# Softmax and window sums of the second half shared between VectorE and GpSimd in a gated spectral convolution kernel

## The chip, the cores and the metric

One core of a Trainium2 chip. The metric is the device time of one execution in microseconds. The engines are TensorE (PE in the rows; PEld is its weight load), VectorE (DVE), ScalarE (ACT), GpSimd (POOL) and SyncE (SP). Each works through its own list of instructions in order; semaphores tie them together.

## The reference

```python
# x: 32 images, 128 channels, 16 x 16
x = x + kan_gate(gn(x))              # gate per image and channel from the mean over pixels
z = gn(x)                            # group norm again
r = conv1x1(relu(conv1x1(relu(conv1x1(z, rw_fc1)), rw_conv)), rw_fc2)
routeing = softmax(r.mean((2, 3)).reshape(B, NF=4, MED=256), axis=1)
s = conv3x3(relu(conv3x3(z, sp_fc1)), sp_fc2)
spatial_routeing = softmax(s.mean((2, 3)).reshape(B, 4, 256), axis=1)
xp = star_scale * relu(z @ w_pw1.T) ** 2 + star_bias
xf = rfft2(xp)
weight         = einsum('bfc,hwf->bhwc', routeing, complex_weights)
spatial_weight = einsum('bfc,hwf->bhwc', spatial_routeing, spatial_weights)
out = xp * spatial_weight + irfft2(xf * weight)
x = x + out @ w_pw2.T
```

The mean over pixels of the second 3x3 convolution is linear, so it needs no convolution: for each of nine taps it needs the sum of the hidden image over the window that the tap sees. That window leaves out an edge row, an edge column or both.

## The kernel before, in words

The 32 images are two halves of 16. A prologue computes group statistics and the gate. Then the branches run over groups of four images (it = 0 to 7): `taps` (L1285) on TensorE are the 3x3 convolution and the first 1x1, ScalarE rectifies them (`conv_hidden`, `route_hidden`, `second_hidden`) and leaves sums over pixels. After a half, its routing is computed:

- `edges` on VectorE (L973 to L975): sums over edge rows and columns, and the corners, of the hidden images.
- `windows` and `window_corners` on VectorE (L987 to L990, L1001): 8 and 4 subtractions of 128 x 8 elements that make the sums of the nine windows.
- `image_sums` (for the second half on ScalarE, L652): copies them, scaled, into the layout that the matmuls read, once for each of two rows of images (g = 0, 1).
- `logits(half)` on TensorE: 32 matmuls of tap pairs (L1350), the last tap (L1354) on partitions 64 to 127, and the route branch (L1357, in the second half L1362) on partitions 0 to 63. ScalarE copies the result out (`logits_copy`), TensorE turns it (`turn_logits`, L1187), VectorE adds the bias (L1046).
- softmax over the four filters: the maximum (L1054), its subtraction, the exponential (ScalarE, L642), the sum (L1064), its reciprocal (L1065), the scaling, and the split of the shares into three bf16 parts (`own_part`, `left_of`).

Then the image loop: one round for each image, `round_of(i)` on each engine. A round of TensorE is, in order, `waves_onto(i)` (L1408), `compose(i-1)` (L1471), `waves_of(i+1)` (L1397), `prime` (L1416), `mix(i+2)` (L1429, L1432), in odd rounds `turn_route` (L1449), `expand(i+3)` (L1384), `reduce(i)` (L1460). VectorE: `products(i)` (L1123, L1124), `even_sum(i+2)` (L1092), `finish(i-2)` (L1128), `terms(i+1)` (L1112 to L1114), `spatial(i+2)` (L1099). ScalarE: `folded_copy(i-1)` (L708, L710), `slot_mix`, in odd rounds `route_copy`, `rectified`, `y_copy(i)`, `square`. GpSimd: `fold(i)` (L457, L458), `unfold(i-2)` (L464, L465), `odd_sum(i+2)` (L451). Rounds 0 to 13 are unrolled and rounds 14 to 29 are in a hardware loop.

The rounds of the first half start while the second half's routing is still to be made. Its steps stand in the unrolled rounds, after the round's own work, at places written by hand: a table `extras` on VectorE and ScalarE, `if` lines on GpSimd and TensorE. Those places set the order, since each engine keeps to it. What waits on them: `products` waits for `waves_onto`; `waves_onto(i)` waits for `terms(i)` and both halves of `fold(i)`; `spatial(i)` waits for `fold(i-1)`; `turn_route(2)`, in round 1, writes bank 7 and so waits for `folded_copy(0)`, which reads it.

In the second half `logits(1)` writes the convolution part to columns 0 to 255 of bank 6 and the route part to columns 256 to 511 of the same bank. The two run on different partitions of the array's rows, so one waits for the other:

```python
if half:
    last.then_inc(conv_logits, 1)
    pe.wait_ge(conv_logits, 1)
    for f in range(NF):
        last = mm(bank[6][NB * f:NB * f + NB, MED:2 * MED], r2_p[:, :], rwf_t[:, f, :], start=True, stop=True)
```

## Time and profile before

| | us |
|---|---|
| median of 3 runs | 253.31 |
| the 3 runs | 251.72 to 256.84 |
| the profiled execution | 252.96 |
| its span, first to last instruction | 251.2 |
| TensorE busy | 230.0 (92%) |
| VectorE busy | 203.2 (81%) |
| ScalarE busy | 147.4 (59%) |
| GpSimd busy | 125.3 (50%) |

The times of the rows count from the start of the span. The profiled execution took 252.96 us as a whole, its span 251.2, so 1.76 us lie around the span. An engine's busy share is a mean over stages with different limits: the branches up to about 92 us, the unrolled rounds to about 172, the loop after them.

### The profile page before, as it was taken

What the parts mean: (1) busy time and instruction counts of PE and PEld (TensorE: products, weight loads), DVE (VectorE), ACT (ScalarE), POOL (GpSimd) and SP (SyncE); (2) the same over time, 40 slices, a digit from 0 to 9 for tenths busy, and PEclk for the clock granted to TensorE, in tenths of its full rate; (3) what the DMA queues carried; (4) which work ended last, traced back from release to release, by engine and by line L of the source; (5) the groups of instructions that cost most, each with busy time, mean ns of one, the idle gap of its engine ahead of it and who ended that gap; (6) DMA issues with size and microseconds to landing.
All of it is one profiled execution on the core that took longest, in us unless ns stands there. A gap on an engine that the chain in (4) does not pass through costs nothing.

```text
span 251.2 us, 6925 instructions
## 1 busy us (share of the span) xinstructions
PE 230.0 (92%) x2257; PEld 180.9 (72%) x2257; DVE 203.2 (81%) x534; ACT 147.4 (59%) x359; POOL 125.3 (50%) x213
## 2 busy tenths in 40 slices
PE   0597889999999999959999989999999999999994
PEld 0597755555444545848788888998989898989983
DVE  3988999982967824886499899899898989989873
ACT  2034386845974866646365756766666675756641
POOL 1532360220000011635467677988686868778771
PEclk9999999999999999979999999999999999999999
DMA  7999500000000000000000010100101010101011
GB/s 214 361 301 274 237 3 3 1 1 3 3 3 0 3 0 1 4 1 22 14 29 23 21 44 22 44 23 30 37 21 42 21 42 21 42 21 42 23 42 63
DMA packets 9483, 13.19 MB, mean 52 GB/s; under 512 B 732, under 2 KB 8924, under 8 KB 9332
## 3 DMA queue, kind: packets, MB, share of 16 engines
q1 hardware_dynamic: 9428, 12.80, 16.1%
q8 instruction: 14, 0.23, 0.4%
q10 hardware_dynamic: 32, 0.08, 0.3%
q14 instruction: 9, 0.07, 0.1%
HBM read 8.69 MB, written 4.19 MB: 51 GB/s over the span
## 4 chain that ended last, share of the span: by engine, by line
PE 71%; DVE 14%; issue 5%; DMA 3%; POOL 3%; ACT 3%; SPq 1%; DVEq 0%; ACTq 0%; POOLq 0%
PE bank L1285 19%; PE bank L1408 10%; PE bank L1460 10%; PE bank L1397 9%; PE bank L1384 7%; PE bank L1471 4%; DMA x_all<-in_x 3%; PE bank L1416 2%; PE bank L1217 1%; PE bank L1350 1%; PE bank L1300 1%; PE bank L1449 1%; DVE x_all L1128 1%; DVE stats L814 1%; PE bank L1429 1%
## 5 line engine op out<-in xcount | busy, mean ns | idle before, releaser
L451 POOL TENSOR_TENSOR eo<-xp 128x256 f32<-128x256 f32 x32 | 23.7, 739 | 70.0 <-ACT xp L682 70.0
L1285 PE MATMUL bank<-z_all,split_h 128*64 128x480 f16 (+2 forms) x320 | 37.5, 374 | 1.0 <-ACT z_all L573 1.0
L1408 PE MATMUL bank<-later_sb,qt_eo 128*128 128x128 f32 x256 | 35.1, 279 | 1.9 <-DVE bank L1113 1.4
L1460 PE MATMUL bank<-later_sb,prod 128*128 128x128 f32 x256 | 34.8, 280 | 0.4 <-DVE prod L1124 0.4
L1397 PE MATMUL bank<-later_sb,eo 128*128 128x128 f32 x256 | 33.9, 276 | 0.0
L1408 PEld LDWEIGHTS bank<-later_sb,qt_eo 128*128 128x128 f32 x256 | 31.3, 192 | 3.6 <-DVE bank L1113 2.0
L1460 PEld LDWEIGHTS bank<-later_sb,prod 128*128 128x128 f32 x256 | 31.8, 196 | 1.4 <-DVE prod L1124 0.6
L689 ACT ACTIVATE w_slot<-bank 128x512 f32<-128x512 f32 x32 | 19.1, 597 | 22.5 <-PE bank L1432 22.5
L1397 PEld LDWEIGHTS bank<-later_sb,eo 128*128 128x128 f32 x256 | 31.1, 192 | 0.4 <-issue 0.4
L457 POOL TENSOR_TENSOR qt_eo<-qt 128x256 f32<-128x256 f32 x32 | 28.5, 890 | 3.3 <-PE bank L1408 2.6
L1285 PEld LDWEIGHTS bank<-z_all,split_h 128*64 128x64 f16 x320 | 17.3, 110 | 16.1 <-issue 3.1
L458 POOL TENSOR_TENSOR qt_eo<-qt 128x256 f32<-128x256 f32 x32 | 28.6, 894 | 0.0
L1128 DVE SCALAR_TENSOR_TENSOR x_all<-x_all,coef,waves 128x256 f32 (+1 forms) x31 | 27.7, 893 | 1.0 <-POOL waves L465 1.0
L1099 DVE SCALAR_TENSOR_TENSOR qt<-xp,shift,bank 128x512 f32<-128x512 f32 x32 | 23.5, 733 | 5.0 <-PE bank L1429 3.6
L675 ACT ACTIVATE relu_v<-bank,relu_scale 128x512 f32<-128x512 f32 x32 | 22.0, 688 | 4.5 <-PE bank L1384 3.7
L1123 DVE TENSOR_TENSOR prod<-bank,t_im 128x256 f32<-128x256 f32 x32 | 13.5, 422 | 13.6 <-PE bank L1408 13.4
L1217 PE MATMUL bank<-early_sb 128*128 128x128 f32 x102 | 15.5, 311 | 9.2 <-DMA x_all<-in_x 9.2
L1384 PE MATMUL bank<-split_h,z_all 128*128 128x256 f16 x128 | 23.4, 279 | 0.0
L1112 DVE TENSOR_TENSOR bank<-bank,w_slot 128x504 f32<-128x504 f32 x32 | 21.7, 679 | 1.0 <-PE bank L1416 0.9
L708 ACT ACTIVATE folded<-bank,coef 128x128 f32<-128x128 f32 x31 | 11.4, 366 | 18.0 <-PE bank L1471 17.7
L1092 DVE SCALAR_TENSOR_TENSOR eo<-xp,shift 128x256 f32<-128x256 f32 x32 | 19.1, 598 | 3.3 <-ACT xp L682 3.3
L1114 DVE TENSOR_TENSOR t_im<-bank,w_slot 128x504 f32<-128x504 f32 x32 | 21.3, 667 | 0.0
(188 smaller groups left out, 470.1 us busy)
## 6 DMA issues: line engine op xcount, KB each, us to landing
x_all<-in_x SPq DMA_DIRECT2D x8, 512.0 KB, 9.0
out<-x_all SPq DMA_DIRECT2D x32, 128.0 KB, 1.7
sp_t<-in_branch_s SPq DMA_DIRECT2D x1, 2560.0 KB, 15.9
later_sb<-in_later SPq DMA_DIRECT2D x1, 918.5 KB, 9.1
sym_all<-in_sym SPq DMA_DIRECT2D x1, 292.5 KB
early_sb<-in_early SPq DMA_DIRECT2D x1, 278.0 KB, 3.8
rwf_t<-in_branch_r SPq DMA_DIRECT2D x1, 256.0 KB, 13.6
kan_sb<-in_kan ACTq DMA_DIRECT2D x1, 80.8 KB, 3.5
```

The lines of the kernel that those rows point to most:

```text
L451: pool.tensor_tensor(eo[p][:, 1, :], xp[p][:, 0, :], xp[p][:, 1, :], ALU.subtract).then_inc(odd_ready, 1)
L457: pool.tensor_tensor(qt_eo[:, 0, :], qt[:, 0, :], qt[:, 1, :], ALU.add).then_inc(q_folded, 1)
L458: pool.tensor_tensor(qt_eo[:, 1, :], qt[:, 0, :], qt[:, 1, :], ALU.subtract).then_inc(q_folded, 1)
L675: act.activation(relu_v[:, :], bank[0], ACT.Relu, scale=relu_scale[:, 0:1]).then_inc(relu_ready, 1)
L1099: dve.scalar_tensor_tensor(out=qt[:, :, :], in0=xp[p], scalar=shift[:, 0:1], in1=mixed_pixel, op0=ALU.add, op1=ALU.mult).then_inc(qt_ready, 1)
L1112: tt(total[:, :, :, 2:P], spec[:, :, :, 2:P], w[:, :, 0, 2:P].unsqueeze(2).broadcast_to(wide_shape), ALU.mult).then_inc(re_ready, 1)
L1128: dve.scalar_tensor_tensor(out=one(x_all, i), in0=one(x_all, i), scalar=one(coef[:, 0, :].unsqueeze(2), i), in1=waves[:, :, :].rearrange(" ...
L1285: last = mm(dst[:, :, rows_out, cols_out], w[:, t, :], pixels(z_all[:, b:b + 2, part, :])[:, :, rows_in, cols_in], start=(n == 0 and t in ...
L1384: last = mm(bank[0][:, t * MED:(t + 1) * MED], z[:, part, cols], w, start=(n == 0), stop=(n == 2))
L1397: last = mm(spec[:, m, :, 64 * odd:64 * odd + 64], eo[p][:, odd, m * P:(m + 1) * P], forward[:, odd, :, :], start=True, stop=True)
L1408: last = mm(total[:, m, :, 64 * odd:64 * odd + 64], qt_eo[:, odd, m * P:(m + 1) * P], forward[:, odd, :, :], start=False, stop=(odd == 1 a ...
L1460: last = mm(bank[1][:, odd * C:(odd + 1) * C], prod[:, m, odd].rearrange("p a s -> p (a s)"), pw2_t[:, m, :], start=(m == 0), stop=(m == 1))
```

## The change

For the second half alone:

- VectorE's `edges(7, 8)` moves from the end of round 0 to just ahead of `spatial(1)`, which precedes round 0. The 8 subtractions of `windows` and the 4 of the corners go from VectorE to GpSimd: 8 between `odd_sum(1)` and `odd_sum(2)`, 4 between `fold(1)` and `odd_sum(3)`. `fold(0)` now stands ahead of `odd_sum(1)`.
- ScalarE copies both rows of images (`image_sums(0)`, `image_sums(1)`) at the end of round 0. The second stood at the end of round 1.
- `logits(1)` writes the route part to bank 7, each of its matmuls beside one of the last tap's, which stays in bank 6. The wait between them is gone. New are waits for `folded_copy(1)` and the third route copy ahead of `logits(1)`, and one for both logits copies ahead of `compose(2)` in round 3.
- The maximum is found at the end of round 4 and no longer of round 3. GpSimd takes it off in one operation, and no longer two. The exponential comes in round 5 (was 6). The sum over the filters is made by two additions on GpSimd in its round 7 (was a reduction on VectorE in round 6), the reciprocal stays on VectorE and comes after round 8 (was 6), and both scalings come on GpSimd in its round 9 (were in 7 and 8).

The diff, cut:

```diff
+        def window_sums(half):
+            its = slice(half * NIT // 2, (half + 1) * NIT // 2)
+            sums, bar = win[:, :, :, its, :], bars[:, :, :, its, :]
+            r, c = rows[:, its], cols_sum[:, its]
+            for k, e in ((0, 1), (2, 0)):
+                yield sums[:, 1, k], (sums[:, 1, 1], c[:, :, :, e])
+                yield sums[:, k, 1], (sums[:, 1, 1], r[:, :, :, e])
+                for ex in range(2):
+                    yield bar[:, e, ex], (r[:, :, :, e], corners[:, its, :, e, ex])
...
@@ gpsimd
-            def off_greatest(q):
+            def off_greatest():
                 pool.wait_ge(max_found, 1)
...
+            def sums():
+                pool.wait_ge(soft_exp, 2)
+                halves = rt_res[:, 0:16, :].rearrange("p (q f) b -> p q f b", f=2)
+                pool.tensor_tensor(halves, by_filter[:, :, 0:2], by_filter[:, :, 2:4], ALU.add).then_inc(sum_found, 1)
+                pool.wait_ge(sum_found, 1)
+                pool.tensor_tensor(rt_max[:, 0], halves[:, :, 0], halves[:, :, 1], ALU.add).then_inc(sum_found, 1)
...
+            def windows():
+                pool.wait_ge(edges_set, 6)
+                pool.wait_ge(s1_ready, 2 * NIT)
+                for out, less in window_sums(1):
+                    steps.did(pool.tensor_tensor(out, less[0], less[1], ALU.subtract))
+
+            def corner_windows():
+                steps.settle()
+                for out, less in window_corners(1):
+                    pool.tensor_tensor(out, less[0], less[1], ALU.subtract).then_inc(win_done, 1)
...
             for i in range(2, HALF - 2):
                 fold(i)
                 unfold(i - 2)
-                if i in (4, 5):
-                    off_greatest(i - 4)
-                if i in (7, 8):
-                    shares(i - 7)
+                if i == 5:
+                    off_greatest()
+                if i == 7:
+                    sums()
+                if i == 9:
+                    shares(0)
+                    shares(1)
@@ scalar
-            extras = {0: lambda: image_sums(0), 1: lambda: image_sums(1), 2: lambda: logits_copy(1), 6: lambda: exponentials(1),
+            extras = {0: both_sums, 2: lambda: logits_copy(1), 5: lambda: exponentials(1),
@@ vector
-            extras = {0: last_windows, 3: greatest, 6: lambda: routing(1, (0,))}
+            extras = {3: lambda: logits(1), 4: greatest, 8: sum_inverse}
@@ tensor
                 if half:
                     pe.wait_ge(r2_ready, 2 * NIT)
+                    pe.wait_ge(folded_ready, 4)
+                    pe.wait_ge(rt_out, 3)
...
-                if half:
-                    last.then_inc(conv_logits, 1)
-                    pe.wait_ge(conv_logits, 1)
-                    for f in range(NF):
-                        last = mm(bank[6][NB * f:NB * f + NB, MED:2 * MED], r2_p[:, :], rwf_t[:, f, :], start=True, stop=True)
+                    last = mm(bank[7 if half else 4][NB * f:NB * f + NB, 0:MED], r2_p[:, :], rwf_t[:, f, :], start=True, stop=True)
...
                 waves_onto(i, h)
+                if unrolled and i == 3:
+                    pe.wait_ge(copied, 4)
```

GpSimd before, from `odd_sum(0)` to `odd_sum(4)`. L451 is `odd_sum`, L457 and L458 are `fold`, L464 and L465 `unfold`.

```order
L451 TENSOR_TENSOR eo0<-xp0 128x256
L451 TENSOR_TENSOR eo1<-xp1 128x256
L457 TENSOR_TENSOR qt_eo<-qt 128x256
L458 TENSOR_TENSOR qt_eo<-qt 128x256
L451 TENSOR_TENSOR eo0<-xp0 128x256
L457 TENSOR_TENSOR qt_eo<-qt 128x256
L458 TENSOR_TENSOR qt_eo<-qt 128x256
L451 TENSOR_TENSOR eo1<-xp1 128x256
```

And now, with `odd_sum` at L471, `fold` at L477 and L478, and the subtractions of `windows` (L511) and of the corners (L516).

```order
L478 TENSOR_TENSOR qt_eo<-qt 128x256
L471 TENSOR_TENSOR eo1<-xp1 128x256
L511 TENSOR_TENSOR win<-win,cols_sum 128x8
L511 TENSOR_TENSOR win<-win,rows 128x8
L511 TENSOR_TENSOR bars<-rows,corners 128x8 x2
L511 TENSOR_TENSOR win<-win,cols_sum 128x8
L511 TENSOR_TENSOR win<-win,rows 128x8
L511 TENSOR_TENSOR bars<-rows,corners 128x8 x2
L471 TENSOR_TENSOR eo0<-xp0 128x256
L477 TENSOR_TENSOR qt_eo<-qt 128x256
L478 TENSOR_TENSOR qt_eo<-qt 128x256
L516 TENSOR_TENSOR win<-win,bars 128x8 x4
```

Eight small subtractions now stand ahead of `odd_sum(2)` and `fold(1)`, and four more ahead of `odd_sum(3)`; `fold(0)` has changed places with `odd_sum(1)`.

TensorE before, at the end of round 2: `reduce(2)`, the tap pairs, the last tap and the route part, then `waves_onto(3)`.

```order
L1460 MATMUL bank1<-later_sb,prod 128x128 x4
L1350 MATMUL bank6<-sp_t,win_p 32x256 x16
L1354 MATMUL bank6<-sp_t,win_p 32x256 x4
L1362 MATMUL bank6<-rwf_t,r2_p 32x256 x4
L1408 MATMUL bank5<-later_sb,qt_eo 128x2x64 x4
```

And now, as far as the first two of four pairs, where L1385 is the last tap and L1387 the route part.

```order
L1485 MATMUL bank1<-later_sb,prod 128x128 x4
L1381 MATMUL bank6<-sp_t,win_p 32x256 x16
L1385 MATMUL bank6<-sp_t,win_p 32x256
L1387 MATMUL bank7<-rwf_t,r2_p 32x256
L1385 MATMUL bank6<-sp_t,win_p 32x256
L1387 MATMUL bank7<-rwf_t,r2_p 32x256
```

The count of matmuls is the same; last tap and route part alternate, in two banks. These lists count a float32 matmul once where the trace shows two.

## Rows read from the trace of the kernel before

**Rows 1.** The page, busy us (share) and instructions by engine.

```profile
PE 230.0 (92%) x2257; PEld 180.9 (72%) x2257; DVE 203.2 (81%) x534; ACT 147.4 (59%) x359; POOL 125.3 (50%) x213
```

**Rows 2.** Busy time in four stretches: us, busy us by engine, granted clock, DMA.

```profile
110.59:113.62 3.03, 3.03 (x17) 2.70 (x18) 1.42 (x4) 1.41 (x3) 0.81 (x2) 0.53 0.01 3
124.27:126.00 1.73, 1.73 (x20) 1.67 (x17) 1.48 (x5) 1.54 (x3) 0.86 (x2) 1.00 0.22 76
121.08:167.34 46.26, 44.82 (x410) 40.32 (x407) 43.05 (x87) 30.33 (x71) 34.82 (x57) 1.00 0.09 29
167.34:201.79 34.45, 34.45 (x322) 31.34 (x322) 31.40 (x65) 22.18 (x52) 26.81 (x41) 1.00 0.09 31
```

**Rows 3.** TensorE timeline, rounds 1 to 3: start us, us, operation, idle before.

```profile
105.06 1.06 PE L1408 MATMUL bank<-later_sb,qt_eo 128*128 128x128 f32 x8
...
110.59 0.41 PE L1449 MATMUL bank<-ident_b,rt_cols 128*128 128x128 bf16 x2 [2.81 <-ACT folded L710]
...
113.62 1.06 PE L1408 MATMUL bank<-later_sb,qt_eo 128*128 128x128 f32 x8
...
119.79 0.64 PE L1354 MATMUL bank<-sp_t,win_p 64*32 64x256 f32 x8
...
120.51 0.64 PE L1362 MATMUL bank<-rwf_t,r_p 64*32 64x256 f32 x8
...
121.08 1.16 PE L1408 MATMUL bank<-later_sb,qt_eo 128*128 128x128 f32 x8
...
122.52 0.49 PE L1187 MATMUL bank<-early_sb,by_image 128*128 128x128 f32 x3
```

**Rows 4.** TensorE timeline, logits of the first half.

```profile
73.34 0.40 PE L1354 MATMUL bank<-sp_t,win_p 64*32 64x256 f32 x1
...
73.35 0.40 PE L1357 MATMUL bank<-rwf_t,r_p 64*32 64x256 f32 x1
...
73.93 2.27 PE L1285 MATMUL bank<-z_all,split_h 128*64 128x512 f16 x20
```

**Rows 5.** VectorE timeline, round 0.

```profile
100.06 0.93 DVE L1092 SCALAR_TENSOR_TENSOR eo<-xp,shift 128x256 f32<-128x256 f32 x1
...
105.87 0.20 DVE L973 TENSOR_REDUCE rows<-s_all 128x4 f32<-128x64 f32 x1
...
106.35 0.63 DVE L987 TENSOR_TENSOR win<-win,cols_sum 128x8 f32<-128x8 f32 x1
...
108.65 0.39 DVE L1001 TENSOR_TENSOR win<-win,bars 128x8 f32<-128x8 f32 x4
```

**Rows 6.** ScalarE timeline, end of round 0.

```profile
109.22 0.58 ACT L652 ACTIVATE win_p<-win 64x32 f32<-64x32 f32 x3 [3.06 <-DVE win L1001]
...
109.94 0.35 ACT L708 ACTIVATE folded<-bank,coef 128x128 f32<-128x128 f32 x1
```

**Rows 7.** VectorE timeline, windows of the first half.

```profile
68.32 0.17 DVE L987 TENSOR_TENSOR win<-win,cols_sum 128x8 f32<-128x8 f32 x1
```

**Rows 8.** GpSimd, groups by shape: busy us, mean ns.

```profile
L442 POOL COPY f_cols<-f_part 128x16 bf16<-128x16 bf16 x12 | 2.7, 274 | 0.1
...
L432 POOL TENSOR_SCALAR f_res<-later_sb,sign 128x8 f32<-128x8 f32 x1 | 0.4, 446 | 0.7 <-DVE coef L914 0.7
```

**Rows 9.** GpSimd timeline, fold(0).

```profile
99.99 0.73 POOL L457 TENSOR_TENSOR qt_eo<-qt 128x256 f32<-128x256 f32 x1
...
100.67 0.91 POOL L458 TENSOR_TENSOR qt_eo<-qt 128x256 f32<-128x256 f32 x1
```

**Rows 10.** TensorE timeline, waves_onto(8).

```profile
145.22 1.16 PE L1408 MATMUL bank<-later_sb,qt_eo 128*128 128x128 f32 x8 [1.18 <-DVE bank L1113]
```

**Rows 11.** VectorE timeline, softmax of the second half.

```profile
127.10 0.60 DVE L1054 TENSOR_REDUCE rt_max<-logit 128x64 f32<-128x256 f32 x1
...
140.93 0.60 DVE L1064 TENSOR_REDUCE rt_max<-logit 128x64 f32<-128x256 f32 x1 [0.64 <-ACT logit L642]
...
141.57 0.55 DVE L1065 RECIPROCAL rt_max<-rt_max 128x64 f32<-128x64 f32 x1
```

More of the change, by code:

```diff
@@ L1004, in window_corners, with windows @@
+            def windows():
+                steps.settle()
+                for out, less in window_sums(0):
+                    steps.did(tt(out, less[0], less[1], ALU.subtract))
+                steps.settle()
+                corner_sums = list(window_corners(0))
+                for n, (out, less) in enumerate(corner_sums):
+                    last = tt(out, less[0], less[1], ALU.subtract)
+                    if n < 3:
+                        steps.did(last)
                 last.then_inc(win_done, 1)
@@ L1144, in _ @@
             even_sum(1, 1)
+            edges(7, 8)
             spatial(1, 1)
```

109 lines of the change are left out of this document (46 added, 63 removed).

## The prediction

> **What bounds the kernel now.** I read the busy line first: TensorE is busy for 230.0 of 251.2 us, so what can be won is its idle time, its time at half clock, and work it needn't do [rows 1]. Next the busy time by stage: in the loop of the second half TensorE never stops. Rounds 13 to 20 take 34.45 us, all of it busy, so one round costs 4.306 us [rows 2]. That is the price of a round when nothing disturbs it. The unrolled rounds that the change touches cost more, and TensorE's timeline shows where, as waves_onto (L1408) opens a round [rows 3]:
> - Round 1 runs from 105.06 to 113.62, 8.56 us. TensorE idles 2.81 us before turn_route (L1449), which waits for folded_copy(0) on ScalarE. The granted clock from 110.59 to 113.62 is then 0.53, near its 1.2 GHz level, and turn_route, expand and reduce take 3.03 us. At 1.00, in round 4, the same three take 1.73 us [rows 2].
> - Round 2 has logits(1). Its last tap takes 0.72 us and the route part another 0.57 us, one behind the other (119.79, 120.51, 121.08) [rows 3]. In the first half the same 16 matmuls, in two banks, start 0.01 us apart and are over in 0.59 us (73.34 to 73.93) [rows 4].
> - Rounds 3 to 12 take 46.26 us [rows 2]. Ten undisturbed rounds are 43.06, and turn_logits, which the others lack, takes 0.60 by its row (L1187) [rows 3], some 0.15 of it over the next matmul's start; so 2.8 us are lost.
> Then who releases the 2.81 us wait: VectorE's edges and windows run from 105.87 to 109.04 [rows 5], ScalarE's image_sums(0) starts at 109.22 and ends when folded_copy(0) starts, 109.94 [rows 6]. Much of VectorE's time there is waiting for GpSimd, which is busy with its own halves at that moment: L987 takes 0.63 us, and 0.17 us in the first half, when GpSimd was idle [rows 5, 7].
>
> **The sum's base.** The profiled execution took 252.96 us, 1.76 outside its span; the median of the runs shown is 253.31, 0.35 above it. I work against 252.96 and add 0.35 at the end.
>
> **Part 1, the windows go to GpSimd.** Off VectorE: 12 small subtractions, 2.7 us of 3.17; edges (3 instructions, 0.46 us, from 105.87 to 106.35) move ahead of spatial(1), where VectorE waited anyway. On GpSimd: 8 subtractions between odd_sum(1) and odd_sum(2), 4 between fold(1) and odd_sum(3). The trace has none of this shape on GpSimd. From below: VectorE does four in 0.39 us, 0.10 each [rows 5]. From above: one 128x8 operation on GpSimd took 0.446 us [rows 8]. The nearest row is L442, 16 elements, 12 in 2.7 us, so 0.22 each; I take that.
> The walk, all on GpSimd's order: as before it is through with fold(0) and odd_sum(1) at 101.58, in whatever order (100.67 plus 0.91) [rows 9]. Edges follow even_sum(1), which ends at 100.99 [rows 5], so they are done at about 101.5. Windows 8 x 0.22: 103.4. odd_sum(2), 0.7: 104.1. fold(1), 0.7 and 0.9 [rows 9]: 105.7. The corners 4 x 0.22: 106.6. On ScalarE both image_sums now stand in round 0, 2 x 0.72 [rows 6]: 108.1. folded_copy(0) and its landing, 0.65 (109.94 to 110.59) [rows 3, 6]: 108.7. So turn_route starts 1.9 us earlier than at 110.59.
> What is queued behind: waves_onto(1) needs fold(1), which ends at 105.7 where TensorE would start the second half of waves_onto at 105.5, so it is 0.2 us late; TensorE reached turn_route at 107.78 before (110.59 less 2.81) and now does at about 107.9 to 108.0, still ahead of 108.7, so this lies inside the wait. spatial(2) on VectorE waits for fold(1) too and ends at about 106.4, where it ended at 105.87; the products behind it came after the windows, at 109.0, and now come at about 106.5. image_sums(1) leaves round 1, where it stood behind y_copy(1): nothing waited for it there.
> **First term: 1.9 us** (at 0.10 each turn_route would start at 107.3, so TensorE's own arrival bounds the gain at 2.8; at 0.446 it would start at 111.4, a loss of 0.8).
>
> **Part 2, the clock.** An idle of 2.81 us was followed by granted 0.53 [rows 2, 3]. An idle of 1.18 us before 145.22 [rows 10] was not: the stretch 121.08 to 167.34 has 1.00 [rows 2]. The new wait is about 0.8 us (107.9 to 108.7), with some 0.8 in two pieces around waves_onto(1), whose first half waits for fold(1) too. I take the clock as staying: **1.3 us** (3.03 less 1.73).
>
> **Part 3, the route part in bank 7.** 1.29 us (119.79 to 121.08) become 0.59 [rows 3, 4]: **0.7 us**. The new waits of logits(1), for folded_copy(1) and route copy 2, are met: mix(4) ahead of it already waits for that copy, and folded_copy(1) comes in early round 2. The new wait ahead of compose(2) is for ScalarE's two copies of logits, twice 0.35 to 0.5 us by folded_copy's 0.35 for half the columns [rows 6], and waves_onto(3), 1.06 us, lies before it [rows 3]: nothing, or 0.2.
>
> **Part 4, rounds 3 to 12.** VectorE's maximum (0.60 us, L1054) moves from the end of round 3 to that of round 4. Its sum (0.60, L1064) and the wait for the exponential before it (0.64) are gone; the reciprocal (0.55) moves from round 6 to 8 [rows 11]. The exponential on ScalarE moves from round 6 to 5. In round 7 TensorE idled 1.18 us before waves_onto(8) for VectorE [rows 10]; 1.8 us less stand ahead of it on VectorE, and the reciprocal isn't there, so this goes. But VectorE has 31.40 of 34.45 us busy in undisturbed rounds [rows 2], a slack of 0.38 a round, so 0.60 takes two rounds to recover, and the reciprocal costs again in rounds 8 to 10: there GpSimd waits for it ahead of shares, with odd_sum(11) and fold(10) queued behind, which I see 0.3 us late at waves_onto(10). GpSimd's added work (its two sums, an estimate of 0.45 and 0.3 from 0.73 for 256 elements [rows 9], now 128 and 64) has waits to lie in: it is busy 26.81 of 34.45 us. Of 2.8 us lost I take **1.2 us** back (ends: nothing, and 2.8).
>
> **Sum.** 1.9 + 1.3 + 0.7 + 1.2 = 5.1. 252.96 less 5.1 is 247.9; with 0.35, 248.2 us.
>
> **Rivals.**
> A. The clock falls all the same, since TensorE's three short idles of round 1 lie close together. Against it: the 1.18 us idle. 248.2 + 1.3 = 249.5.
> B. Rounds 3 to 12 give nothing: VectorE runs behind from the logits on, and the reciprocal and GpSimd's waits replace the stall. For it: 0.38 us of slack a round is thin. 249.4.
> C. They give all 2.8: 246.6. For it: VectorE's wait of 0.64 and the sum both go, and the rest is spread over three rounds.
> D. A small operation on GpSimd costs 0.446. Then turn_route is at 111.4, the clock falls as before: 248.2 + 2.7 + 1.3 = 252.2, no change.
> E, the slower side. Each small subtraction on GpSimd waits out VectorE's operations on two SBUF tensors, as VectorE's waited out GpSimd's: 0.63 for 0.17 [rows 5, 7]. turn_route then starts at 108.7 + 12 x (d - 0.22). Against before it decides from 110.59 + 0.7 + 1.2 = 112.5, so from d = 0.54. At 0.66: 114.0, and 253.31 + 3.4 - 1.9 = 254.8. Against it: VectorE has only even_sum of that kind in the stretch, some 0.5 us of 4. That the stall only changes its name is within D and E.
> A rule speaks against the change as a whole: the Trainium skill (GPSIMD Engine Reference, Engine selection and Key points) sends elementwise work to VectorE, calling GpSimd about two times slower for two inputs, and says that the two contend where VectorE has two SBUF inputs. The trace agrees on both: 0.22 against 0.10, and 0.63 for 0.17. By the first statement (an estimate from that page, twice VectorE's 0.10) turn_route would start at 108.5; the second would make it rival E.
>
> **How the numbers follow.** Forecast 45 in 100, A 12, B 18, C 15, D 6, E 4. 2% is 5.1 us, about what a measurement of this kernel can tell from no change, and the forecast lies on it (248.24). Faster by over 2%: half of the forecast, C, and some of A and B where another term is larger: 0.44. Slower: E, 0.04. Within: 0.52. The range leaves out E, half of D, and the ends of C: 246.4 to 251.2.
>
> **What would show it.** Right: turn_route of round 1 at 108.4 to 109.2 with under 1.3 us idle and granted clock 1.00 behind it; the 12 subtractions at 0.15 to 0.3 us; last tap and route part paired in 0.6 us; waves_onto(3) at about 117.2; rounds 3 to 12 in 44.5 to 45.7 us. Wrong: GpSimd's subtractions over 0.35 us, the granted clock again near 0.5 in round 1, or rounds 3 to 12 above 46 us, with TensorE waiting for fold or for VectorE's terms in rounds 8 to 11.

## The result and the profile after

The changed kernel takes 246.19 us (median of 4 runs, 246.10 to 249.94), the kernel before beside it 255.07 (251.72 to 257.28). The ratio is 0.976 [0.973, 0.980], so the change makes the kernel 2.4% faster. The prediction was 248.2 us, a ratio of 0.980 to its own 253.31, at the edge of that interval; the time itself lies 0.2 us below the range. The profiled execution took 246.10 us with a span of 244.3, against 252.96 and 251.2: 6.9 us less, where 5.1 were predicted. By the ratio the gain is some 6 us (0.024 of about 252.5), at least in part because the profiled execution of the kernel before is one that lost time to the clock, and not all of them do (the run with GpSimd at the late place shows it). The ratios here and below leave out executions that a slower prologue lengthened (the last section shows one); where a profiled execution had it, stretches are compared by their length.

The page of the changed kernel: its busy line, the granted clock in 40 slices, and the chain that ended last.

```profile
PE 228.7 (94%) x2257; PEld 180.8 (74%) x2257; DVE 198.0 (81%) x521; ACT 147.6 (60%) x359; POOL 128.6 (53%) x226
...
PEclk9988999999999999999999999999999999999999
...
PE 88%; DVE 5%; DMA 3%; ACT 2%; issue 1%; SPq 1%; ACTq 0%
```

The chain on the page of the kernel before:

```profile
PE 71%; DVE 14%; issue 5%; DMA 3%; POOL 3%; ACT 3%; SPq 1%; DVEq 0%; ACTq 0%; POOLq 0%
```

TensorE has as many instructions as in [rows 1]. The chain has moved onto it: VectorE's share fell from 14% to 5%, and GpSimd's went although GpSimd now does more. The only slices below full clock lie in the prologue; the one of round 1 is gone.

TensorE's timeline, the places of [rows 3]: waves_onto (L1433) opens a round, turn_route is L1474, the last tap L1385, the route part L1387.

```profile
100.42 1.16 PE L1433 MATMUL bank<-later_sb,qt_eo 128*128 128x128 f32 x8
...
104.45 1.18 PE L1433 MATMUL bank<-later_sb,qt_eo 128*128 128x128 f32 x8
...
108.03 0.32 PE L1474 MATMUL bank<-ident_b,rt_cols 128*128 128x128 bf16 x2 [0.74 <-ACT folded L751]
...
109.73 1.06 PE L1433 MATMUL bank<-later_sb,qt_eo 128*128 128x128 f32 x8
...
115.90 0.40 PE L1385 MATMUL bank<-sp_t,win_p 64*32 64x256 f32 x1
115.91 0.40 PE L1387 MATMUL bank<-rwf_t,r_p 64*32 64x256 f32 x1
...
116.49 1.16 PE L1433 MATMUL bank<-later_sb,qt_eo 128*128 128x128 f32 x8
```

Stretches of the changed kernel that answer to the first and the last two of [rows 2] (span from:to, us, busy us of PE, PEld, DVE, ACT and POOL, granted clock, DMA):

```profile
108.03:109.73 1.70, 1.70 (x17) 1.64 (x17) 1.46 (x4) 1.41 (x3) 0.80 (x2) 1.00 0.00 0
...
116.49:160.46 43.97, 43.97 (x414) 39.97 (x407) 40.48 (x86) 30.36 (x71) 36.05 (x58) 1.00 0.09 30
160.46:194.90 34.44, 34.44 (x322) 31.37 (x322) 31.41 (x65) 22.19 (x52) 26.80 (x41) 1.00 0.09 31
```

So the 6.9 us can be laid out by place:

| stretch | before | after | gained | predicted |
|---|---|---|---|---|
| up to turn_route of round 1 | 110.59 | 108.03 | 2.56 | 1.9 |
| turn_route to waves_onto(2) | 3.03 | 1.70 | 1.33 | 1.3 |
| round 2 (with the logits) | 7.46 | 6.76 | 0.70 | 0.7 |
| rounds 3 to 12 | 46.26 | 43.97 | 2.29 | 1.2 |
| the eight undisturbed rounds behind them | 34.45 | 34.44 | 0.0 | 0 |
| sum | | | 6.9 | 5.1 |

In rounds 3 to 12 TensorE's busy time is now the whole stretch; before it was 44.82 of 46.26.

### The profile page after: what moved, and what is told of

The parts are those of the page before. It is cut to its first block, busy times and chain, and to the rows that moved or that the text cites. A ratio compares the mean times of both kernels' runs of the same rounds, so it can differ in the third digit from the quotient of the medians.

```text
span 244.3 us, 6928 instructions
## 1 busy us (share of the span) xinstructions
PE 228.7 (94%) x2257; PEld 180.8 (74%) x2257; DVE 198.0 (81%) x521; ACT 147.6 (60%) x359; POOL 128.6 (53%) x226
## 3 DMA queue, kind: packets, MB, share of 16 engines
HBM read 8.69 MB, written 4.19 MB: 53 GB/s over the span
## 4 chain that ended last, share of the span: by engine, by line
PE 88%; DVE 5%; DMA 3%; ACT 2%; issue 1%; SPq 1%; ACTq 0%
PE bank L1314 21%; PE bank L1485 12%; PE bank L1433 12%; PE bank L1422 11%; PE bank L1409 9%; PE bank L1496 5%; PE bank L1246 3%; PE bank L1441 3%; DMA x_all<-in_x 3%; PE bank L1474 2%; PE bank L1329 2%; PE bank L1381 2%; PE bank L1454 1%; DVE stats L859 1%; ACT z_all L614 1%
## 5 line engine op out<-in xcount | busy, mean ns | idle before, releaser
L471 POOL TENSOR_TENSOR eo<-xp 128x256 f32<-128x256 f32 x32 | 24.4, 762 | 62.6 <-ACT xp L723 62.4
L1433 PE MATMUL bank<-later_sb,qt_eo 128*128 128x128 f32 x256 | 34.6, 277 | 0.0
L1485 PE MATMUL bank<-later_sb,prod 128*128 128x128 f32 x256 | 34.1, 276 | 0.4 <-DVE prod L1160 0.4
L477 POOL TENSOR_TENSOR qt_eo<-qt 128x256 f32<-128x256 f32 x32 | 29.2, 912 | 7.3 <-DVE qt L1135 5.3
L1433 PEld LDWEIGHTS bank<-later_sb,qt_eo 128*128 128x128 f32 x256 | 31.3, 192 | 1.1 <-issue 0.6
L1485 PEld LDWEIGHTS bank<-later_sb,prod 128*128 128x128 f32 x256 | 31.1, 192 | 1.4 <-DVE prod L1160 0.6
L478 POOL TENSOR_TENSOR qt_eo<-qt 128x256 f32<-128x256 f32 x32 | 28.1, 877 | 0.0
L1246 PE MATMUL bank<-early_sb 128*128 128x128 f32 x102 | 16.7, 327 | 9.0 <-DMA x_all<-in_x 9.0
L1409 PE MATMUL bank<-split_h,z_all 128*128 128x256 f16 x128 | 22.9, 274 | 0.0
L1246 PEld LDWEIGHTS bank<-early_sb 128*128 128x128 f32 x102 | 15.4, 237 | 9.0 <-issue 9.0
L749 ACT ACTIVATE folded<-bank,coef 128x128 f32<-128x128 f32 x31 | 11.4, 367 | 16.3 <-PE bank L1496 16.0
```

The source lines that it names most:

```text
L471: pool.tensor_tensor(eo[p][:, 1, :], xp[p][:, 0, :], xp[p][:, 1, :], ALU.subtract).then_inc(odd_ready, 1)
L477: pool.tensor_tensor(qt_eo[:, 0, :], qt[:, 0, :], qt[:, 1, :], ALU.add).then_inc(q_folded, 1)
L478: pool.tensor_tensor(qt_eo[:, 1, :], qt[:, 0, :], qt[:, 1, :], ALU.subtract).then_inc(q_folded, 1)
L1246: mm(bank[1][:, 0:P], group, ident, start=True, stop=True)
L1409: last = mm(bank[0][:, t * MED:(t + 1) * MED], z[:, part, cols], w, start=(n == 0), stop=(n == 2))
L1433: last = mm(total[:, m, :, 64 * odd:64 * odd + 64], qt_eo[:, odd, m * P:(m + 1) * P], forward[:, odd, :, :], start=False, stop=(odd == 1 a ...
```

## The experiments

Each kernel was profiled and timed against the kernel before, whose medians beside them were 252.6 to 252.7 us. A round is the time from one waves_onto to the next on TensorE's timeline. The pieces of the change first, each put alone on the kernel before.

### The windows alone

```diff
 before.py
@@ gpsimd
-            odd_sum(1, 1)
             fold(0)
+            odd_sum(1, 1)
+            windows()
             odd_sum(2, 0)
             fold(1)
+            corner_windows()
@@ scalar
-            extras = {0: lambda: image_sums(0), 1: lambda: image_sums(1),
+            extras = {0: both_sums,
@@ vector
             even_sum(1, 1)
+            edges(7, 8)
             spatial(1, 1)
```

> The kernel before with part 1 alone: the second half's 12 subtractions on GpSimd, edges ahead of spatial(1), both image_sums in round 0. Theory (the four gains are separate and add up): round 1's turn_route starts at 108.0 (before 110.59), the granted clock behind it is 1.00, waves_onto(2) starts at 109.7 (before 113.62), and rounds 3 to 12 still take 46.3 us, so the span is 251.2 - 3.9 = 247.3. Rival (the rounds behind give a part back, since VectorE's maximum and sum now meet a TensorE that is 3.9 us further on): rounds 3 to 12 over 47 us and a span of 248 or more.

Measured: ratio 0.986 [0.981, 0.992], span 247.2. turn_route starts at 107.95 after 0.74 us of idle, round 0 takes 4.03 and round 1 5.28 us (before 4.20 and 8.56), the granted clock stays at 1.00. Round 2 is as before (7.46), rounds 3 to 12 take 46.12. waves_onto(2) comes at 109.65, where it came at 113.62: all of the first two terms, 3.9 us in the table above and 4.0 here, comes from this piece, and nothing later changes with it.

### The bank alone

```diff
 before.py
-                    if not half:
-                        last = mm(bank[4][NB * f:NB * f + NB, 0:MED], r2_p[:, :], rwf_t[:, f, :], start=True, stop=True)
-                if half:
-                    last.then_inc(conv_logits, 1)
-                    pe.wait_ge(conv_logits, 1)
...
+                    last = mm(bank[7 if half else 4][NB * f:NB * f + NB, 0:MED], r2_p[:, :], rwf_t[:, f, :], start=True, stop=True)
```

> The kernel before with part 3 alone: the route part of the second half's logits in bank 7, beside the last tap. Theory: last tap and route part over in 0.6 us where they took 1.29, the span 250.5 (0.7 less). Rival (the new wait ahead of compose(2) costs what the pairing gives): TensorE idle before compose(2), span 251.2.

Measured: ratio 0.996 [0.992, 0.999]. Round 2 takes 6.77 us for 7.46; rounds 0, 1 and 3 to 12 are those of before (4.19, 8.57, 46.10). The piece is worth 0.7 us, and the added waits cost nothing.

### The softmax alone

```diff
 before.py
@@ gpsimd
-                if i in (4, 5):
-                    off_greatest(i - 4)
-                if i in (7, 8):
-                    shares(i - 7)
+                if i == 5:
+                    off_greatest()
+                if i == 7:
+                    sums()
+                if i == 9:
+                    shares(0)
+                    shares(1)
@@ scalar
-                      6: lambda: exponentials(1)
+                      5: lambda: exponentials(1)
@@ vector
-            extras = {0: last_windows, 3: greatest, 6: lambda: routing(1, (0,))}
+            extras = {0: last_windows, 3: lambda: logits(1), 4: greatest, 8: sum_inverse}
```

> The kernel before with part 4 alone: maximum after round 4, exponential in round 5, sums on GpSimd in round 7, reciprocal after round 8, scaling in GpSimd's round 9. Theory (the gain in rounds 3 to 12 is the softmax's own): rounds 3 to 12 take 44.0 us where they took 46.26, span 248.9. Rival (rounds 3 to 12 gained because the parts ahead let VectorE come in better step): rounds 3 to 12 at 45 us or more, span 250 or more.

Measured: ratio 0.991 [0.988, 0.994], span 248.5. Rounds 3 to 12 fall from 46.10 to 43.80 us; rounds 1 and 2 keep 8.52 and 7.46. All the gain of the fourth term is this piece's, and none of it is owed to the earlier windows. The three pieces give 4.0, 0.7 and 2.3 us, together 7.0 where the whole change gives 6.9.

### The idle filled, nothing moved

To take the clock's share out of the wait's, TensorE gets work that nothing reads, where it idled.

```diff
 before.py
+                if unrolled and i == 1:
+                    pe.wait_ge(relu_ready, i + 3)
+                    for _ in range(12):
+                        mm(bank[0], ident_b[:, :], filters[:, :], start=True, stop=True)
                 if j:
                     turn_route(pair + 2, half)
```

> The kernel before, with 12 matmuls of 512 bf16 columns, whose result nothing reads, on TensorE in round 1 ahead of turn_route, in the time in which it idles 2.81 us. Theory (the clock falls after the idle time, and costs 1.3 us by itself): the granted clock from turn_route to waves_onto(2) is 1.00, the three steps take 1.73 us, waves_onto(2) starts at 112.3 where it started at 113.62, span 249.9. Rival (the clock falls there for another reason, or the added matmuls run over): granted clock near 0.5 again, or waves_onto(2) at 113 or later, span 251 or more.

Measured: ratio 0.997 [0.994, 0.999]. The timeline from turn_route (L1449) on; it all stands 3.8 us later than in [rows 3], as the start of round 0 does (104.68):

```profile
108.87 1.06 PE L1408 MATMUL bank<-later_sb,qt_eo 128*128 128x128 f32 x8
...
114.42 0.31 PE L1449 MATMUL bank<-ident_b,rt_cols 128*128 128x128 bf16 x2
...
116.12 1.06 PE L1408 MATMUL bank<-later_sb,qt_eo 128*128 128x128 f32 x8
```

turn_route comes 5.55 us after waves_onto(1), as before (5.53), so the wait is still there with work in it. But turn_route to waves_onto(2) takes 1.70 us and no longer 3.03. The profiled execution of the kernel before lost 1.3 us to the lower clock behind the wait, beside the wait itself. The ratio shows less, 0.9 us (0.2 to 1.5), and the run with GpSimd late says why: not every execution loses them.

### How much waiting the clock bears

Twelve more subtractions of 128 x 8 on GpSimd, into a tensor that nothing reads, beside the twelve of the changed kernel:

```diff
 after.py
@@ windows
                 for n, (out, less) in enumerate(window_sums(1)):
                     steps.did(pool.tensor_tensor(out, less[0], less[1], ALU.subtract))
+                    steps.did(pool.tensor_tensor(spare[:, n], less[0], less[1], ALU.subtract))
@@ corner_windows
+                    steps.did(pool.tensor_tensor(spare[:, 8 + n], less[0], less[1], ALU.subtract))
```

> The changed kernel with each of GpSimd's 12 subtractions made twice, the second into a tensor that nothing reads: 24 instead of 12, 0.17 us each, so 2.0 us more ahead of image_sums. Theory of the prediction's walk (turn_route starts at a fixed time plus 12 x d, d the cost of one): d of 0.34, corners done at 107.5, turn_route at about 110.0, 2.0 us later, clock again below 1.00 behind it, span 246.5 to 247.6. Rival (part of the 2.0 is hidden): turn_route under 109.3, the clock 1.00, span under 245.6.

Measured: ratio 0.982 [0.976, 0.989], span 245.9. TensorE's timeline (turn_route is L1477), and its windows:

```profile
105.25 1.30 PE L1436 MATMUL bank<-later_sb,qt_eo 128*128 128x128 f32 x8 [1.02 <-POOL qt_eo L478]
...
109.61 0.31 PE L1477 MATMUL bank<-ident_b,rt_cols 128*128 128x128 bf16 x2 [1.39 <-ACT folded L754]
```

```profile
103.00:108.00 5.00, 3.98 (x37) 3.52 (x34) 3.06 (x7) 2.54 (x8) 5.00 (x18) 1.00 0.01 2
108.00:113.00 5.00, 3.61 (x37) 3.37 (x33) 3.91 (x7) 3.98 (x13) 2.51 (x5) 1.00 0.01 2
```

Counted from the start of round 0, turn_route comes 9.57 us on, where it came 7.61: 1.96 more, and 12 x 0.17 is 2.0. The prediction's formula, a place on GpSimd's list times twelve, holds. The clock does not fall: two idles, of 1.02 and 1.39 us in the same round, with 1.00 granted over both windows. That goes further against rival A than the change itself, whose one idle was 0.74.

### GpSimd at the late place, VectorE at the early one

Two kernels that separate the engine from the place. First the subtractions stay on GpSimd but wait, with the edges, until VectorE has finished round 0, as before:

```diff
 after.py
@@ gpsimd
             odd_sum(1, 1)
-            windows()
             odd_sum(2, 0)
             fold(1)
+            windows()
             corner_windows()
@@ vector
             even_sum(1, 1)
-            edges(7, 8)
             spatial(1, 1)
...
-            extras = {3: lambda: logits(1), 4: greatest, 8: sum_inverse}
+            extras = {0: lambda: edges(7, 8), 3: lambda: logits(1), 4: greatest, 8: sum_inverse}
```

> The changed kernel with edges and the 12 subtractions late again, but on GpSimd: edges on VectorE at the end of round 0, the subtractions on GpSimd between fold(1) and odd_sum(3). Both image_sums stay in round 0. With the kernel before (VectorE, late), the changed kernel (GpSimd, early) and the run with VectorE early this closes a square of engine and place. Theory (the place gives the gain): edges end at 105.4, 12 x 0.17 on GpSimd to 107.5, image_sums to 109.2, turn_route at 109.9 after more than 2 us idle, the granted clock behind it low again, waves_onto(2) at 111.6 to 112.9, span 246.2 to 247.5. Rival (the engine gives it): turn_route before 108.7, span under 245.

Measured: ratio 0.990 [0.985, 0.995], span 247.6. turn_route (L1473) and waves_onto(2) (L1432) on TensorE's timeline, and the windows around them:

```profile
109.74 0.32 PE L1473 MATMUL bank<-ident_b,rt_cols 128*128 128x128 bf16 x2 [3.55 <-ACT folded L751]
...
112.06 1.92 PE L1432 MATMUL bank<-later_sb,qt_eo 128*128 128x128 f32 x8
```

```profile
108.00:113.00 5.00, 3.26 (x21) 3.23 (x22) 0.75 (x1) 3.75 (x12) 2.13 (x4) 0.78 0.00 2
113.00:118.00 5.00, 5.00 (x48) 4.29 (x51) 3.97 (x8) 2.54 (x7) 3.22 (x5) 0.88 0.09 28
```

Round 1 takes 8.59 us, as long as before (8.56), and the clock falls after the idle of 3.55 us; here the low stretch reaches into round 2, which takes 7.78 us for 6.76.

The fall doesn't come in every execution. Of the ten executions of this kernel four have a mean granted clock of 1.000 over the whole span and took 248.2 to 248.8 us; three have 0.992 or 0.993 and took 249.4 to 249.8, the profiled one among them; three have 0.986 and took 251.1 to 251.5. The kernel before splits in the same way. Beside these experiments 16 of its executions have a mean of 0.997 or more, with a median of 251.4 us, and 18 have 0.991 to 0.993, with a median of 252.75; three more have 0.986, at 254.1 to 254.2. The profiled one has 0.991. The first two medians lie 1.4 us apart, about the 1.3 of the clock term, and with the idle filled ten executions lie between 250.9 and 251.8. So the same wait is followed by low clock in some executions and not in others. That the difference lies behind this wait is inferred, as no trace of an execution without the fall was kept; the mean alone doesn't tell, since the changed kernel took 246.10 us both with 0.993, its clock being lower in the prologue, and with 1.000. What the executions at 0.986 lose beyond that stays open.

Then the subtractions go back to VectorE, but stay early:

```diff
 after.py
@@ gpsimd
             odd_sum(1, 1)
-            windows()
             odd_sum(2, 0)
             fold(1)
-            corner_windows()
@@ vector
             even_sum(1, 1)
             edges(7, 8)
+            windows(1)
             spatial(1, 1)
```

> The changed kernel with the 12 subtractions on VectorE again, but at the new place, ahead of spatial(1), where GpSimd's odd_sum(1) and then nothing runs beside them. Theory (the place gave the gain, the engine little): the 12 take 1.2 to 1.6 us, spatial(1) and products(0) come that much later, and with it waves_onto(1) by under 1 us; turn_route at about 108.0 to 108.7, span 244.3 to 245.1. Rival (the engine gave it): the subtractions wait for GpSimd, 0.63 us each for some, spatial(1) is 2.5 us late, TensorE idles before reduce(0) and waves_onto(1), span 246.5 or more.

Measured: ratio 0.974 [0.968, 0.981], span 244.4. Three of VectorE's rows for it (each line gives the start, the time, and x4 for four in a row):

```profile
101.04 0.17 DVE L1015 TENSOR_TENSOR win<-win,cols_sum 128x8 f32<-128x8 f32 x1
101.12 0.16 DVE L1015 TENSOR_TENSOR win<-win,rows 128x8 f32<-128x8 f32 x1
...
101.80 0.40 DVE L1019 TENSOR_TENSOR win<-win,bars 128x8 f32<-128x8 f32 x4
```

The twelve take 1.16 us in all, where they took 2.7 beside a busy GpSimd [rows 5]. They put off spatial(1), to 102.11 for 101.11, and what stands behind it on VectorE, but not fold(1), which starts at 102.93 for 103.45. Rounds 0 and 1 take 4.61 and 5.05, together 0.35 us more than in the changed kernel (9.66 to 9.31), yet turn_route comes at 108.19 and the times can't be told apart.

| subtractions | late | early |
|---|---|---|
| on VectorE | 12.76 (the kernel before) | 9.66 |
| on GpSimd | 12.61, and 1.0 more in round 2 | 9.31 (the change) |

The table has rounds 0 and 1 together, in us. The place gave the gain, over 3 us on either engine; the engine gives 0.35 at most. Part of the place's gain is the clock's: without the time lost to the fall in the two late profiles (1.3 us on VectorE, 0.6 and the 1.0 of round 2 on GpSimd) it is 1.8 us on VectorE and 2.7 on GpSimd.

### The order of fold(0) and odd_sum(1)

```diff
 after.py
@@ gpsimd
-            fold(0)
             odd_sum(1, 1)
+            fold(0)
             windows()
```

> The changed kernel with odd_sum(1) ahead of fold(0) on GpSimd, as it was before. The prediction took this swap as worth nothing. Theory (it is worth 0.3 to 0.5 us at the start of round 0 and nothing at turn_route's end, since ScalarE bounds that): waves_onto(0) at 100.86 for 100.42, turn_route at 108.0 to 108.3, span 244.3 to 244.6. Rival (GpSimd's chain bounds it): everything behind comes 0.5 us later, turn_route at 108.5, span 244.8.

Measured: ratio 0.976 [0.969, 0.983], span 244.6. waves_onto(0) idles 0.34 us for fold(0) again, and turn_route comes at 108.28. Rounds 0 and 1 together stay the same (9.30). So the swap gives some 0.3 us, by the start of round 0 and nowhere else, below what the times show. It rests on the idle row: in the nine profiled executions with fold(0) first, round 0 begins anywhere from 99.45 to 100.66, here at 100.68.

### The second image_sums back to round 1

In the changed kernel ScalarE, no longer GpSimd, is the last link before turn_route (the rows are in the next section). This undoes one part of the change:

```diff
 after.py
@@ scalar
-            extras = {0: both_sums,
+            extras = {0: lambda: image_sums(0), 1: lambda: image_sums(1),
```

> The changed kernel, with image_sums(1) back at the end of round 1 on ScalarE. In the changed kernel image_sums(0) starts at 105.67 when ScalarE's own square(3) ends, and both take 1.68 us ahead of folded_copy(0). Theory (ScalarE's queue now bounds turn_route, no longer the subtractions): turn_route comes 0.74 us earlier, its wait is gone, waves_onto(2) starts at 109.0 (109.73 in the changed kernel), span 243.6. Rival (logits(1) then waits for image_sums(1), as its four copies end only shortly before): idle time before L1381's matmuls, span 244.3 or more.

Measured: ratio 0.970 [0.961, 0.979], 245.02 us, span 243.3. turn_route (L1470) waits for nothing:

```profile
107.03 0.34 PE L1470 MATMUL bank<-ident_b,rt_cols 128*128 128x128 bf16 x2
```

Round 1 falls from 5.28 to 4.51 us, rounds 2 and 3 to 12 are unchanged (6.76, 43.81). Moving image_sums(1) forward, a part of the change, cost 0.8 us: nothing needs it before the logits in round 2, and it stood in ScalarE's list ahead of the copy that TensorE waited for.

### The sum over filters back on VectorE

```diff
 after.py
@@ gpsimd
-                if i == 7:
-                    sums()
@@ vector, sum_inverse
-                dve.wait_ge(sum_found, 2)
+                dve.wait_ge(soft_exp, 2)
+                steps.then(dve.tensor_reduce(sm, by_filter.rearrange("p q f b -> p q b f"), AX, ALU.add))
```

> The changed kernel with the sum over the filters back on VectorE as a reduction, right ahead of the reciprocal after round 8, so that GpSimd's two sums of round 7 are gone. Theory (what gave the 2.3 us of rounds 3 to 12 is that VectorE no longer waits for the exponential and has its three extra steps rounds apart, not that GpSimd sums): rounds 3 to 12 take 43.8 to 44.1 us, span 244.3 to 244.6. Rival (VectorE's 0.38 us of slack a round can't take 0.60 and 0.54 at once): TensorE waits for VectorE's terms in round 9 or 10, rounds 3 to 12 at 44.4 us or more, span 244.9 or more.

Measured: ratio 0.982 [0.979, 0.986], span 245.1. Rounds 3 to 12 take 44.59 us for 43.81. VectorE's rows of the sum and the reciprocal, then TensorE's waves_onto (L1425) of rounds 10 and 13:

```profile
143.46 0.59 DVE L1097 TENSOR_REDUCE rt_max<-logit 128x64 f32<-128x256 f32 x1
144.08 0.55 DVE L1098 RECIPROCAL rt_max<-rt_max 128x64 f32<-128x64 f32 x1
```

```profile
147.47 1.31 PE L1425 MATMUL bank<-later_sb,qt_eo 128*128 128x128 f32 x8 [0.20 <-DVE bank L1141]
...
161.00 1.13 PE L1425 MATMUL bank<-later_sb,qt_eo 128*128 128x128 f32 x8 [0.20 <-DVE bank L1141]
```

With both behind one another TensorE waits for VectorE again, and once more three rounds later. So GpSimd's two additions are worth 0.8 us, by taking 0.6 us off VectorE in the one round that has the reciprocal. Engine and place are not separated here: a reduction on VectorE in a round of its own, as the maximum has, was not run.

### The maximum back to round 3

```diff
 after.py
@@ vector
-            extras = {3: lambda: logits(1), 4: greatest, 8: sum_inverse}
+            extras = {3: logits_greatest, 8: sum_inverse}
```

> The changed kernel with the maximum back at the end of round 3, right behind the logits, as before. Theory (spreading the steps gave a part of its own): VectorE is 0.6 us later at products(4) and products(5), waves_onto(5) and (6) wait as in the kernel before, where rounds 4 and 5 took 4.80 and 4.48 us; rounds 3 to 12 at 44.3 to 44.6, span 244.8 to 245.1. Rival (only the missing wait for the exponential counted): rounds 3 to 12 stay at 43.8, span 244.3.

Measured: ratio 0.979 [0.976, 0.983]. Rounds 4 and 5 take 4.47 and 4.49 us for 4.21 and 4.39, rounds 3 to 12 together 44.18, so 0.37 more. The span is that of the changed kernel (244.3), since round 0 began 0.35 us earlier in this execution (100.07), and the time doesn't show it. Spreading the logits' bias and the maximum over two rounds is worth 0.4 us.

### One subtraction where there were two

On top of the kernel with image_sums(1) in round 1: GpSimd's left_of for both parts of the filters in one operation.

```diff
-                    left_of(i - 10, 0)
-                    left_of(i - 10, 1)
+                    left_of(i - 10)
```

> The changed kernel with image_sums(1) back in round 1, and GpSimd's left_of made in one operation of 128x256 for each part where it was two of 128x128. Round 11 still takes 4.62 us against 4.38 undisturbed, since fold(11) stands behind left_of(0) on GpSimd. One operation of this size costs 0.7 us, two of half the size 0.99. Theory: fold(11) comes 0.3 us earlier, round 11 at 4.4 us, span 243.0 to 243.1 (243.3 without it). Rival (left_of waits for ScalarE's own part and the merged one ends no earlier where it counts): round 11 at 4.6, span 243.3.

Measured: ratio 0.973 [0.969, 0.977], 244.88 us. On GpSimd the one takes 0.67 us:

```profile
148.20 0.67 POOL L525 TENSOR_TENSOR rt_res<-logit,rt_cols 128x256 f32<-128x256 f32 x1 [0.46 <-ACT rt_cols L701]
```

Round 11 takes 4.51 us for 4.62, rounds 3 to 12 43.64 for 43.81. These 0.2 us are seen in the rounds, not in the times. Both kernels with image_sums(1) in round 1 have the lowest medians of the study, 1.2 and 1.3 us below the changed kernel's; 0.8 and 0.9 of that is seen in the rounds. They beat the kernel before, and can't be told apart from each other. That they beat the changed kernel is shown by the rounds; the intervals of the ratios touch or overlap (0.961 to 0.979 and 0.969 to 0.977, for 0.973 to 0.980).

## Why the prediction was right in kind, and where it fell short

**Part 1, the wait at turn_route: 2.56 for 1.9, and the last link was another.** GpSimd's list from odd_sum(1) on in the changed kernel (L471 odd_sum, L511 windows, L477 and L478 fold(1), L516 corners):

```profile
100.25 0.91 POOL L471 TENSOR_TENSOR eo<-xp 128x256 f32<-128x256 f32 x1
101.27 0.20 POOL L511 TENSOR_TENSOR win<-win,cols_sum 128x8 f32<-128x8 f32 x1
...
102.58 0.91 POOL L471 TENSOR_TENSOR eo<-xp 128x256 f32<-128x256 f32 x1
103.45 0.72 POOL L477 TENSOR_TENSOR qt_eo<-qt 128x256 f32<-128x256 f32 x1
...
104.81 0.69 POOL L516 TENSOR_TENSOR win<-win,bars 128x8 f32<-128x8 f32 x4
```

And ScalarE's behind it (L723 square, L693 image_sums, L749 folded_copy):

```profile
104.93 0.62 ACT L723 ACTIVATE xp<-relu_v 128x512 f32<-128x512 f32 x1
105.67 0.58 ACT L693 ACTIVATE win_p<-win 64x32 f32<-64x32 f32 x3
...
107.12 0.21 ACT L693 ACTIVATE r_p<-r_sum 64x8 f32<-64x8 f32 x1
107.35 0.37 ACT L749 ACTIVATE folded<-bank,coef 128x128 f32<-128x128 f32 x1
```

| step of the walk | predicted | measured |
|---|---|---|
| windows begin | 101.5 | 101.27 |
| eight windows done | 103.4 | 102.58 (1.31 us, 0.16 each) |
| odd_sum(2) done | 104.1 | 103.45 |
| fold(1) done | 105.7 | 104.81 |
| corners done | 106.6 | 105.50 (0.69 us, 0.17 each) |
| both image_sums done | 108.1 | 107.35 |
| turn_route | 108.7 | 108.03 |

The failed size is the 0.22 us that the prediction took from an operation of 16 elements: a subtraction took 0.16 to 0.17, which is 0.6 us over twelve. GpSimd's fold(1) at 1.36 us for 1.6 and the earlier start gave 0.5 more, and odd_sum(2) at 0.87 for 0.7 took 0.2 back. The walk was also rounded up on its way: its terms from 101.5 on add up to 108.5, not 108.7. And counted from the start of round 0 the gain is 2.12 us; the other 0.44 is an earlier start, of which fold(0)'s idle of 0.34 is one part and the scatter of that start another. Against it stands what the walk left out: ScalarE has work of its own in that place. square(3) ended at 105.55, after the corners, and the two image_sums took 1.68 us and not 1.44. So a smaller price of the subtractions would have gained nothing more: with the twelve done on VectorE by 102.2, turn_route still came at 108.19. At the prediction's lower end, 0.10 each, it saw turn_route at 107.3; the bound is ScalarE's list. That image_sums(1) forward costs nothing ("nothing waited for it there") was true of its old place and wrong of its new one; taking it back gave 0.8 us. fold(1) late for waves_onto(1) was right: that row has 1.18 us for 1.06.

**Part 2, the clock: right, 1.33 for 1.3.** The idle was 0.74 us, the clock 1.00 behind it. The filled idle gives the same 1.3 in its profiled execution, so the term is shown, and the cause with it: full speed where TensorE had worked, about half behind the idle of 2.81 us (granted 0.53), a fall a little later behind that of 3.55 (waves_onto(2) in 1.92 us for 1.06), none behind 1.02, 1.18 and 1.39. Rival A is refuted. What the prediction didn't see is that the kernel before pays these 1.3 us in some executions only, so they count in full in the spans compared here and in part in the ratio.

**Part 3, the bank: right, 0.70 for 0.7**, by the change and by the bank alone. Last tap and route part start 0.01 us apart, and 115.90 to 116.49 is the 0.59 of [rows 4].

**Part 4, rounds 3 to 12: 2.29 for 1.2.** The step that failed is the cost put on what stays on VectorE: "0.60 takes two rounds to recover, and the reciprocal costs again in rounds 8 to 10", with waves_onto(10) 0.3 us late. In the changed kernel odd rounds from 5 on take 4.39 us and even ones 4.21 to 4.24, the undisturbed mean of 4.30 in rounds 4 to 10, maximum and reciprocal included. Only round 3 (4.93, with turn_logits) and round 11 (4.62) are longer: 0.54 and 0.23 over 4.39. Round 10, where the 0.3 us were expected, is 0.03 longer than the other even ones. The reason is in VectorE's groups for rounds 3 to 12, before and after; the line is even_sum (times, busy us, mean ns):

```profile
L1092 DVE SCALAR_TENSOR_TENSOR eo<-xp,shift 128x256 f32<-128x256 f32 x10 | 7.1, 714 | 0.0
```

```profile
L1128 DVE SCALAR_TENSOR_TENSOR eo<-xp,shift 128x256 f32<-128x256 f32 x10 | 5.2, 516 | 0.0
```

The same instruction costs 0.2 us a round less on the average. In the kernel before, even_sum took 0.89 to 0.98 us in rounds 4, 5, 7, 8 and 9, and those five rounds are the ones that the changed kernel shortened by more than 0.05 (they lasted 4.80, 4.48, 5.73, 4.35 and 4.48 us); in the other five rounds it took 0.47 to 0.60. In the changed kernel its longest is 0.70. Two moments show how. Before, in round 5, where VectorE is late, GpSimd's fold (L457) is first:

```profile
132.54 0.73 POOL L457 TENSOR_TENSOR qt_eo<-qt 128x256 f32<-128x256 f32 x1
```

```profile
132.67 0.89 DVE L1092 SCALAR_TENSOR_TENSOR eo<-xp,shift 128x256 f32<-128x256 f32 x1
```

After, VectorE's even_sum is first and fold is the one that takes longer:

```profile
131.78 0.48 DVE L1128 SCALAR_TENSOR_TENSOR eo<-xp,shift 128x256 f32<-128x256 f32 x1
```

```profile
131.88 0.96 POOL L477 TENSOR_TENSOR qt_eo<-qt 128x256 f32<-128x256 f32 x1
```

Whoever begins second pays, some 0.4 us for VectorE and 0.2 for GpSimd. GpSimd has waits to lose it in, VectorE has not. In rounds 4 and 7 it was odd_sum, in 5, 8 and 9 fold that had begun first. The prediction read the slack of 0.38 us a round from undisturbed rounds, where VectorE is first. Once VectorE runs late it begins second and pays 0.4 a round, as much as the slack; it came back into step after two and after three such rounds, in which TensorE lost time too. The stall in the kernel before was thus more than the softmax's own work. In the changed kernel no round adds more than about 0.6 us to VectorE, and it never gets into that state. In the run with the sum back on VectorE the first stall is that of 0.59 and 0.55 in one round alone, since even_sum takes 0.71 us there as against 0.70; the second, three rounds on, has it:

```profile
158.19 1.01 DVE L1120 SCALAR_TENSOR_TENSOR eo<-xp,shift 128x256 f32<-128x256 f32 x1
```

```profile
158.19 0.73 POOL L477 TENSOR_TENSOR qt_eo<-qt 128x256 f32<-128x256 f32 x1
```

The longest is in the run with 24 subtractions, where GpSimd ran odd_sum and both halves of fold back to back from 107.03 to 109.12:

```profile
107.26 2.14 DVE L1131 SCALAR_TENSOR_TENSOR eo<-xp,shift 128x256 f32<-128x256 f32 x1
```

The Trainium skill (SBUF — State Buffer, "SBUF: two separate sides") says that a VectorE operation with two SBUF inputs and a GpSimd one that reads SBUF exclude each other, the first holding the ports to its end. The trace agrees in kind (0.48 to 0.89 us, and 0.73 to 0.96); the prediction used that rule for the windows only, where it no longer applied, and not for the rounds, where it decides the slack. That being late feeds itself in this way is read from these rows and is not shown by an experiment: no run changed this contention alone.

What GpSimd pays for the rest, from its timeline (L504 shares, then fold(11)'s second half), and waves_onto(11) on TensorE:

```profile
144.18 0.87 POOL L504 TENSOR_TENSOR logit<-logit,rt_max 128x128 f32<-128x128 f32 x2 [1.03 <-DVE rt_max L1106]
...
151.28 0.72 POOL L478 TENSOR_TENSOR qt_eo<-qt 128x256 f32<-128x256 f32 x1
```

```profile
151.46 1.30 PE L1433 MATMUL bank<-later_sb,qt_eo 128*128 128x128 f32 x8
```

The wait of shares for the reciprocal, which the prediction named, is there, 1.03 us long, and costs those 0.03 us in place of 0.3. In round 11 left_of puts fold(11) back, and waves_onto takes 1.30 us for 1.06; one left_of in place of two brings 0.11 back.

**The rivals.** B (rounds 3 to 12 give nothing) is refuted. C (all 2.8 us, 246.6) came closest: 2.29, and of what is left 0.2 is round 11; the rest was no loss, since the prediction set turn_logits at 0.44 where it costs 0.54, and the stretch of [rows 2] ends 0.16 us behind the start of waves_onto(13). D and E are refuted: a subtraction took 0.20 us by its row. What VectorE ran beside them was mostly spatial and products, which read a bank. E's mechanism exists all the same: in the run with 24, the one subtraction that met even_sum took 0.40 us.

**The rule that spoke against the change.** The Trainium skill (GPSIMD Engine Reference, Engine selection) gives elementwise work on two inputs to VectorE, GpSimd being about two times slower. The trace agrees on the ratio, 0.16 to 0.17 us against 0.08 to 0.10. It did not decide here: for the windows the engine hardly mattered, and for the sums 0.77 us on GpSimd replaced 0.6 on VectorE in the round of the reciprocal and won 0.8, where VectorE's time was short. Whether another round on VectorE would have done as well is open.

## What to carry to other kernels

Before moving work to another engine, ask whether an earlier place on the same one would do: here the place was worth over 3 us (1.8 to 2.7 without the clock's part) and the engine 0.35 at most. Read an engine's slack in the state in which it will be used, since an engine that runs late can lose its slack to contention that it doesn't meet when in step; so small pieces in several rounds can cost less than together in one (0.4 us for the maximum beside the bias, 0.8 for the sum beside the reciprocal). And once a wait is shortened, look at what stands in the waiting copy's own list: the last gain (0.8 us) was in a step that had been moved forward for no reader.
